# Two batches half a step pattern apart: a step-ordered interleaving of the attention stages, and biases added on GpSimd

## The reference, cut to what matters

```python
# stage a (layer 0)
x = layernorm(x + attn(x, Wq, Wk, Wv) @ Wo + bo)       # causal, rotary, 16 query and 4 key/value heads
x = layernorm(x + xattn(x, ctx, segment ids))          # latent keys of 64, rotary part of 64, look back 8
# stage b: experts, stage c: gated delta rule (not touched)
# stage d (layer 1)
q = w8a8_linear(x, wq, bq); k = ctx @ wk.T + bk; v = ctx @ wv.T + bv
o = softmax(q k / sqrt(16) + mask) v
x = layernorm(x + w8a8_linear(o, wo, bo))              # rows of x and of o quantized to 8 bits each
g = softmax(x @ W_gate.T)                              # the best head alone gives k and v to all heads
x = layernorm(x + causal_attention(q heads, k of best head, g_max * v of best head))
```

## Time and profile before

| | |
|---|---|
| time, median of 3 runs | 2388.04 us (2384.26 to 2389.48) |
| profiled execution | 2385.96 us, span 2383.9 us |
| PE busy | 2033.3 us, 85% of the span, 10850 matmuls |
| PEld / DVE / ACT / POOL busy | 1513.1 / 1458.6 / 879.0 / 140.0 us |
| mean granted TensorE clock | 0.896 of full speed |
| phase a, first transpose to last layer norm | 25.9 to 413.3 us |
| phase d, first context transpose to last layer norm | 1997.8 to 2380.7 us |

### The profile page before, as it was taken

How to read it: one execution, slowest core, us unless ns; L and a number is a source line. 1 busy time by engine, 2 the same in 40 slices (tenths; PEclk the granted TensorE clock), 3 DMA queues, 4 the chain that set the end, 5 groups by cost and what they waited for, 6 DMA issues and landing times. The chain is left out here.

```text
span 2383.9 us, 28590 instructions
## 1 busy us (share of the span) xinstructions
PE 2033.3 (85%) x10850; PEld 1513.1 (63%) x10850; DVE 1458.6 (61%) x3251; ACT 879.0 (37%) x1540; POOL 140.0 (6%) x130
## 2 busy tenths in 40 slices
PE   6988988898994979899898998989989884787786
PEld 4867777554552658586685866858668672455464
DVE  3567665223222576867768677676776854767666
ACT  2433433111112535354454534545345431332233
POOL 1011010100002000000000000000000001011010
PEclk8889888899996889999999999999999996777787
DMA  3000000400001120201203012030121202000000
GB/s 128 6 14 10 6 5 5 187 0 9 0 1 66 36 54 14 67 28 36 54 14 79 16 36 54 16 83 10 36 54 27 54 1 69 7 12 14 7 5 5
DMA packets 163259, 78.81 MB, mean 33 GB/s; under 512 B 140530, under 2 KB 152628, under 8 KB 162132
## 3 DMA queue, kind: packets, MB, share of 16 engines
q1 hardware_dynamic: 163124, 76.99, 11.8%
HBM read 59.88 MB, written 16.91 MB: 32 GB/s over the span
## 5 line engine op out<-in xcount | busy, mean ns | idle before, releaser
L1566 DVE TENSOR_TENSOR c_Y<-c_V,c_bank 128x512 f32<-128x512 f32 x192 | 131.8, 686 | 82.3 <-PE c_bank L1239 82.3
L1239 PE MATMUL c_bank<-c_Y,c_NP 128*128 128x128 f32 x1536 | 176.4, 276 | 0.0
L1239 PEld LDWEIGHTS c_bank<-c_Y,c_NP 128*128 128x128 f32 x1536 | 173.9, 192 | 3.4 <-issue 3.4
L1540 DVE SCALAR_TENSOR_TENSOR c_NP<-c_NP,c_cj,c_bank 128x256 f32<-128x256 f32 x256 | 104.8, 475 | 67.0 <-ACT c_NP L1410 67.0
L1172 PE MATMUL c_bank<-c_xT,c_wqk 128*128 128x512 f32 x256 | 127.2, 644 | 5.1 <-ACT c_pad L1366 3.1
L1501 DVE SCALAR_TENSOR_TENSOR c_cv<-c_pad,c_wcqk,c_cv 128x1024 f32<-128x1024 f32 x96 | 122.2, 1280 | 12.0 <-ACT c_cv L1380 11.2
L1501 DVE SCALAR_TENSOR_TENSOR c_cv<-c_pad,c_wcv,c_cv 128x1024 f32<-128x1024 f32 x96 | 122.5, 1283 | 2.6
L1326 PE MATMUL c_bank<-c_wout,c_yT 128*128 128x256 f32 x512 | 121.3, 383 | 0.0
L1172 PE MATMUL c_bank<-c_xT,c_wv 128*128 128x512 f32 x256 | 112.0, 595 | 4.1 <-DVE c_acc L1594 3.6
L1232 PE MATMUL c_bank<-c_wz,c_xT 128*128 128x512 f32 x256 | 111.2, 592 | 0.0
L855 ACT ACTIVATE b_sg<-b_G 128x512 f32<-128x512 f32 x50 | 29.7, 597 | 220.6 <-PE b_G L808 220.5
(11 more groups left out here) (409 smaller groups left out, 4226.6 us busy)
## 6 DMA issues: line engine op xcount, KB each, us to landing
b_wup<-b_in_wup SPq DMA_DIRECT2D x4, 1280.0 KB, 13.5
c_wqk<-c_in_wqk SPq DMA_DIRECT2D x9, 512.0 KB, 3.4
c_wv<-c_in_wv SPq DMA_DIRECT2D x8, 512.0 KB, 3.5
c_wz<-c_in_wz SPq DMA_DIRECT2D x8, 512.0 KB, 4.1
c_wout<-c_in_wout SPq DMA_DIRECT2D x8, 512.0 KB, 3.7
diagonal_blocks<-c_NP SPq DMA_DIRECT2D x64, 64.0 KB
c_A<-diagonal_blocks SPq DMA_DIRECT2D x8, 512.0 KB, 3.4
c_NP<-no_blocks SPq DMA_DIRECT2D x32, 128.0 KB, 3.8
```

Source lines behind the costliest of these rows:

```text
L1239: last = pe.matmul(banks[n % 4][:, b * P:(b + 1) * P], lhsT(h, 4 * q + b), rhs(h, 4 * q + b), start=True, stop=True)
L1540: dve.scalar_tensor_tensor(NP[:, h, bb, :, :], spread(NP[:, h, bb, 1, :], 2), cj[:, h, bb:bb + 1], gp, ALU.mult, ALU.mult).then_inc(s["NP_ ...
L1566: dve.tensor_tensor(rr(Y, h, q), rr(V, h, q), four(banks[n % 4][:, :]), ALU.subtract).then_inc(s["y_ready"], 1)
```

## The change

The step order of `in_turns` is replaced by keys. Each `yield` now names a step number, and `in_step_order` always runs the program whose next key is lowest, where the key is batch number x PERIOD + lane x LAG + step. In phase a a batch has 24 steps, in phase d 28, and the lag of lane 1 is 6.5 in both, so lane 1 is 6.5 steps behind lane 0 on every engine's order: while one lane is in the six steps of an attention, the other is in steps outside it. The start of the next batch follows the end of the last one in the same sequence of keys. SyncE's and GpSimd's instructions get keys too. The steps themselves hold the same instructions as before, with one exception: the biases `bo` of phase a and `bv` of phase d are no longer one-row matmuls. They are loaded as full tiles of 128 rows, and GpSimd adds them, in phase a to the lane's x after it has been transposed (`x_biased`, which `ln1` waits for), in phase d to the copied values (`v_biased`, which the first cross-attention step of TensorE waits for instead of `v_ready`).

```diff
-def in_turns(programs):
-    done = object()
-    running = list(programs)
+def in_step_order(lanes, period, lag, program):
+    def steps(n, L):
+        for i in range(B // LANES):
+            for step in program(i, L):
+                yield i * period + n * lag + step
+    running = [[next(p), n, p] for n, p in enumerate(steps(n, L) for n, L in enumerate(lanes))]
     while running:
-        running = [p for p in running if next(p, done) is not done]
+        first = min(running)
+        first[0] = next(first[2], None)
+        if first[0] is None:
+            running.remove(first)
...
-    def on_tensor(self, pe, i, scores, values):
+    def on_tensor(self, pe, i, scores, values, step):
         w = self.width + 1
         for s in range(QUADS + 2):
+            if s:
+                yield step + s
...
# phase a
+        PERIOD, LAG = 24, 6.5
...
+            def transfers(i, L):
+                more = i < B // LANES - 1
+                if more:
+                    yield 0.9
                     sp.wait_ge(L.xcT_ps, i + 1)
...
+                    yield 10.9
                     sp.wait_ge(L.ln1.step, at(i, L.ln1.DVE_STEPS, 1))
...
+                yield 24.9
+                store_batch(sp, i, i * LANES + L.n, L.ln2.done, L.x2[:, :], x_dst, L.x2_stored, L.x2_free)
...
+            def batch_program(i, L):
+                yield 1
+                pool.wait_ge(L.xcT_ps, i + 1)
+                pool.tensor_tensor(L.xt[:, :], L.xt[:, :], w["bo"][:, :], ALU.add).then_inc(L.x_biased, 1)
+                for c in range(DC):
+                    yield 2 + c
+                    pool.wait_ge(L.qk_ready, i + 1)
...
-                pe.matmul(L.M[:, D:2 * D], ones[:, :], w["bo"][:, :], start=True, stop=False)
...
# phase d
+        PERIOD, LAG = 28, 6.5
...
+            def batch_program(i, L):
+                yield 2
+                pool.wait_ge(L.v_ready, i + 1)
+                pool.tensor_tensor(L.vaug[:, :, 0:HD], L.vaug[:, :, 0:HD], w["bv"][:, :].rearrange("p (h d) -> p h d", h=H), ALU.add)\
+                    .then_inc(L.v_biased, 1)
...
-                pe.matmul(L.T[:, 0:D], ones[:, :], w["bv"][:, :], start=True, stop=False)
```

More of the change, by code:

```diff
@@ L158, in on_tensor, with on_scalar @@
                 last.then_inc(self.o_ready, 1)
-            yield
-    def on_scalar(self, act, i):
+    def on_scalar(self, act, i, step):
         for s in range(QUADS + 1):
+            if s:
+                yield step + s
             if s >= 1:
@@ L210, in __init__, with on_vector @@
         self.done = ph.sem(name + "_done")
-    def on_vector(self, dve, i, out, x, y):
+    def on_vector(self, dve, i, out, x, y, then):
         link = Linked(dve, self.step, self.DVE_STEPS, i)
@@ L505, in lane_program @@
                 last.then_inc(L.y2_ps, 1)
-                yield
-                if more:
-                    yield from start_batch(i + 1, L)
-            in_turns([start_batch(0, L) for L in lanes])
-            for i in range(0, B // LANES - 1):
-                in_turns([lane_program(i, L, True) for L in lanes])
-            in_turns([lane_program(B // LANES - 1, L, False) for L in lanes])
+            in_step_order(lanes, PERIOD, LAG, batch_program)
         @block.scalar
@@ L563, in lane_program @@
                     act.activation(L.latT[:, 4 * half:4 * half + 4, :], four(bank[:, :]), ACT.Copy).then_inc(L.latT_ready, 1)
-                yield
-                if not more:
-                    L.ln2.on_scalar(act, i)
-                    return
-                next_start = start_batch(i + 1, L)
-                next(next_start)
-                yield
-                L.ln2.on_scalar(act, i)
-                yield from next_start
-            in_turns([start_batch(0, L) for L in lanes])
-            for i in range(0, B // LANES - 1):
-                in_turns([lane_program(i, L, True) for L in lanes])
-            in_turns([lane_program(B // LANES - 1, L, False) for L in lanes])
+                yield 24
+                L.ln2.on_scalar(act, i)
+            in_step_order(lanes, PERIOD, LAG, batch_program)
         @block.vector
@@ L1852, in _, with project8 @@
             pe.wait_ge(s["wstep_ready"], 1)
-            def project8(i, L, n, out):
-                yield
+            def project8(i, L, n, out, step):
+                yield step
                 pe.wait_ge(L.xquant.done, at(i, 2, n + 1))
@@ L1938, in self_scores @@
                                      start=False, stop=True)
[L1940 to L1947 removed]
+                yield from L.self_att.on_tensor(pe, i, self_scores, lambda n, h: L.vaug2[:, :], 20)
+            in_step_order(lanes, PERIOD, LAG, batch_program)
         @block.scalar
@@ L2002, in lane_program @@
-                next_start = start_batch(i + 1, L)
-                next(next_start)
-                yield
-                L.ln2.on_scalar(act, i)
-                yield from next_start
-            in_turns([start_batch(0, L) for L in lanes])
-            for i in range(0, B // LANES - 1):
-                in_turns([lane_program(i, L, True) for L in lanes])
-            in_turns([lane_program(B // LANES - 1, L, False) for L in lanes])
+                yield 20
+                yield from L.self_att.on_scalar(act, i, 20)
```

294 lines of the change are left out of this document (141 added, 153 removed).

## The result

The changed kernel takes 2519.47 us (median of 4 runs, 2510.63 to 2521.91), the kernel before 2387.68 (4 runs beside it): a ratio of 1.0547, with a 95% interval of 1.053 to 1.0564. The forecast was slower, 2429, in a range up to 2475. The sign was right; the change cost 132 us where I had 41.

What follows compares the result with a forecast made beforehand. Lockstep attention was taken as dense on TensorE, with gappy chains between. Phase a +40.1, phase d -7.1, load +0.5 and clock +8 gave +41.5 us on 2388.0, so 2429 us, range 2362 to 2475.

Steps and rivals of the forecast that it cites:

- The chains of phase a: phase a's four segments per round, at full clock: 103.2 us against 95.0; with the ends, +40.1 for the phase.
- The halves' chain: phase a, two query halves with rotations, the second waiting for banks the first's rotation reads: 11.4 us per lane.
- the segment whose clock is 0.98: phase a, lane 1's cross-attention until lane 0's next self-attention: forecast at 22.45 us.
- the roots: layer-norm square roots behind ScalarE table loads, delaying VectorE: 1.4 us late in phase a; 0.75, 0.7, 1.5, 1.5 in d.
- lane 0's self-attention: phase a segment from that attention's first score to the next attention's, with lane 1's projections and key expansions: 28.65 us.
- Rival 1: VectorE's insertions between quads (roots, `ln1`, quantization) cost nothing, saving 14.6 us per pair of rounds: 2371 us; 25 in 100.
- about 2 in each of three segments: price charged for VectorE's insertions in phase a, 6 us per round, which would vanish if they cost nothing.
- I take 8: lower-clock allowance over phases a and d: 8 us, between 0 and 14 for two half-clock quads each round.
- rival 2: lower clock holds through lone attentions in phases a and d; half the quads slow gives 2496 us; 12 in 100.
- Phase d: its segments at full clock: 92.15 us per round against 95.55; with the ends, -7.1 for the phase.
- a first maximum 2.7 us late: phase d, lane 0's self-attention: VectorE does quantization, rescaling and both lanes' `ln1` before its first maximum, 2.7 us late.
- Biases: one-row matmuls' absence counted in the segments; GpSimd's additions hidden; full tiles' first load adds 0.5 us in phase d.

Runs made afterwards that it cites:

- kernel 11: the changed kernel with the second query half's first matmul group in free bank O, not waiting for the first half's rotation; 2501.65 us.
- kernels 7 and 10: the changed kernel with copies replacing layer-norm square roots in phases a and d, 2486.36 us; the same plus filler matmuls in phase a, 2455.36 us.
- kernel 10: the changed kernel with unused filler matmuls before three waits of phase a and copies replacing square roots in phases a and d; 2455.36 us.
- kernel 6: the changed kernel with unused filler transposes on TensorE ahead of three waits in phase a; 2504.31 us.

## Why the forecast was right in sign and a third in size

**The chains of phase a** were right in the main. The halves' chain sets its segments (kernel 11), the waits are as long as forecast, and the segment whose clock is 0.98 came out within 0.1 us. The forecast for a was +40.1 at full clock. Part of the agreement is luck: the roots cost 23 us where the segments hold 11, and the terms written down for lane 0's self-attention add up to 29.35, not 28.65. Rival 1's "about 2 in each of three segments" is in two of them only.

**The clock is the step that failed:** "I take 8", from two slow quads a round, with 14 as the upper bound. In phase a alone the slow matmuls add to 69.6 us, and by kernels 7 and 10 most of such time is on the path: 100.3 measured is 40.1 + 60.2. The fillers moved 31 us of it; for the rest, that it lies on the path is argued from them and not shown. The bound was wrong because I counted only scores as slow. Behind a wait there stand a whole query half (2.6 us lost), a first score (0.9), an output projection (0.9). And I did not let the clock fall inside a lone attention. That was rival 2 (2496, 12 in 100): the mechanism was real, in some attentions and not in half of all quads, and deserved more than its small chance. What the forecast named as what would make it wrong, a clock that falls within lone attentions, is what happened.

**Rival 1**, insertions on VectorE that cost nothing, did not hold. Its price of 34 us for phase d was roots (18) and quantization (16). Without the roots d is only 3.9 us shorter, but their waits were there, 12.4 us of TensorE's idle time, and without the quantization in its old place 8.3 us of idle time went too. Slower matmuls filled what either left.

**Phase d** was forecast at -7.1 and measured +26.1: the forecast's sign came from phase a alone. The single term that I can check there, a first maximum 2.7 us late, held: 5.17 instead of 2.73 between quads is 2.4. But each segment was 0.8 to 3.0 us longer than forecast. The same step failed here in another way: the segments are at full clock, so they took for granted that the 41 to 56 us which d's matmuls lost to the clock before would be gone, and the new order lost 61 to 63. Yet fillers inside waits raised the clock to 0.85 and left d as long as it was (412.9), so slow matmuls that they reach are not what sets it. How the 33 us divide between slow cross quads, values and projections on one side and VectorE's rows on the other is open.

**Biases.** I had put them at +0.5 and inside the segments. In lockstep they win 26 us (24 in the traces: 11 in a, 13 in d), in the new order 16. The load of full tiles was not seen.

**Transfers** cost nothing that the trace shows, as forecast: no compute engine waits for a transfer inside phase a or d, and the DMA share stayed at 0.02 and 0.03.

**What is left.** With fillers and without roots the new order still stands 65 us above the kernel before (2453.4 against 2388.27 beside it). In the traces some 50 of it are in phase a (phase b's input at 467.7 in kernel 10, at 418.1 before) and 18 in d (403.9 us against 386.1). Phase a's remaining surplus of 23 is no more than the 21 of the kernel before, so the clock explains little of its 50. What is left there is the structure: lone attentions, halves one after the other, one lane alone at either end. These were not taken apart further.

## What to carry to other kernels

When an order is changed so that one stream's chain is to hide behind another's, price each new wait of 2 to 3 us, as they were here, twice: once as the wait, once for the matmuls behind it at half clock, all of them until it recovers, and not only for the kind of instruction that comes first. If the old order ran partly at half clock, ask too why the new one should not: segments at full clock forecast a gain that d never had. Test it with fillers of unused matmuls inside the wait: if added work makes the kernel faster, it is the clock. Read busy and idle time apart, too: two runs in d shortened the waits and lost it again in slower matmuls, which the total alone hides. And measure the parts of a two-part change apart: here the part that looked like housekeeping was the gain, and with fillers it gave 2345 us where the whole change gave 2519.

## What the runs showed of the hardware that I had not expected

The granted clock fell while TensorE had no gap. The windows view of the third kernel (lockstep, biases on GpSimd), at the end of a self-attention, where only transposes, values of 17 columns and the output projection are left:

```profile
156.00:160.00 4.00, 4.00 (x38) 4.00 (x36) 1.59 (x9) 1.71 (x3) 0.00 (x0) 0.97 0.00 0
160.00:165.00 5.00, 4.97 (x15) 3.39 (x14) 1.74 (x10) 2.05 (x3) 0.00 (x0) 0.50 0.02 5
```

TensorE is busy for all of 156 to 160 and 4.97 of the next 5 us, and the clock goes from 0.97 to 0.50. And in kernel 6 it stayed up over a wait of 2.4 us (234.67 to 237.10) in which TensorE did nothing but 1.04 us of transposes.

The same change of order does not cost the same in each round: two rounds of a with equal instructions took 113.35 us (155.20 to 268.55) and 122.8 us (268.55 to 391.33); the first two segments had clocks of 0.90 and 0.82 in the one, 0.80 and 0.64 in the other. With fillers both took 112.7 (151.42 to 264.12 and on to 376.79).

GpSimd's addition of two 128x256 tiles takes 0.72 us, half again what a quarter of an expansion of 1.9 us suggests. VectorE's 256-column addition beside an expansion took 2.06 instead of 0.42 and ended 0.28 us after it. The Trainium skill ("SBUF — State Buffer", Who interferes with whom) says that a VectorE instruction with two inputs in SBUF blocks while a GpSimd instruction that reads SBUF holds the ports that they share; this trace agrees: the expansion began first, at 2261.72, and the addition ended only behind it.
